# A vision tower on one core: the second stage's attention product turned and spread over four array tiles, squares on ScalarE, bias rows split in the first stage, the last weight fold at its end

## The reference

```python
h = patches(x) @ W.T + b                                    # 768 -> 256
u = layernorm(h); Bu = (u @ W_B.T + b_B) * dt
xs[t] = exp(-exp(log_A) * dt) * xs[t-1] + Bu[t]             # scan over the 196 patches of an image
h = h + xs @ W_C.T + b_C + u @ W_D.T + b_D
x = layernorm(h)
# attention over the 64 images at each patch position, 4 heads of 64
y1 = ln(x + softmax(q @ k.T / 8) @ v @ out_proj.T + ob) * g1 + be1
gates = softmax(y1 @ wg); e = argmax(gates)                 # 8 experts, at most S/8 tokens each, in token order
moe = gate * ((y1 @ w1[e] + b1[e]) @ w2[e] + b2[e])         # 0 for a token past its expert's capacity
out = h + ln(y1 + moe) * g2 + be2
```

## Time and profile before

| | before |
|---|---|
| median of three runs | 1286.43 us (1283.87 to 1287.28) |
| profiled execution | 1285.87 us, span 1284.0 us |
| TensorE busy | 1183.7 us, 92% |
| VectorE busy | 1010.5 us, 79% |
| GpSimd busy | 857.0 us, 67% |
| ScalarE busy | 720.8 us, 56% |
| mean granted TensorE clock | 0.972 |
| stages in the span | first to 547.85, second to 1086.73, third to 1284 |

### The profile page before, as it was taken

The page is one execution under the profiler, slowest core; times in us unless marked ns, Lnnn a source line. Parts: engine busy times, 40 slices in busy tenths (PEclk is TensorE's granted clock), DMA queues, the critical chain, the costliest instruction groups (busy, mean ns, idle before and its releaser), DMA issues. The chain is left out here.

```text
span 1284.0 us, 37111 instructions
## 1 busy us (share of the span) xinstructions
PE 1183.7 (92%) x11134; PEld 1086.1 (85%) x11135; DVE 1010.5 (79%) x2957; ACT 720.8 (56%) x1518; POOL 857.0 (67%) x1159
## 2 busy tenths in 40 slices
PE   1999999999999999749999999999999984999994
PEld 1999999999999999749999999999999973666662
DVE  4688888888888888705778877877788776699997
ACT  3455566566565655415555555555555540678885
POOL 1566666666666666373777777777777773378887
PEclk9999999999999999978999999999999996999997
DMA  7435555545454542211333333333233325788882
GB/s 221 165 126 157 173 155 177 164 146 172 141 184 149 179 148 90 91 42 39 113 104 110 107 107 102 110 105 110 98 111 107 110 92 157 207 236 241 238 235 93
DMA packets 97304, 180.11 MB, mean 140 GB/s; under 512 B 12319, under 2 KB 62753, under 8 KB 96226
## 3 DMA queue, kind: packets, MB, share of 16 engines
q1 hardware_dynamic: 82500, 138.66, 36.0%
q0 software_dynamic: 13312, 39.75, 8.3%
q10 hardware_dynamic: 1440, 1.07, 0.3%
HBM read 112.69 MB, written 67.80 MB: 141 GB/s over the span
## 5 line engine op out<-in xcount | busy, mean ns | idle before, releaser
L528 POOL TENSOR_TENSOR xl<-xf,xh 128x512 fp32r<-128x512 f32 x141 | 183.8, 1332 | 178.0 <-ACT xh L447 178.0
L311 PE MATMUL ps_h<-wh,xh 128*128 128x256 f32 x588 | 166.3, 283 | 4.9 <-DVE xl L669 4.9
L311 PE MATMUL ps_h<-wh,xl 128*128 128x256 f32 x588 | 166.1, 282 | 0.0
L311 PE MATMUL ps_h<-wl,xh 128*128 128x256 f32 x588 | 165.3, 281 | 0.0
L1061 POOL DMA_INDIRECT bins<-rows,slot_i x98 | 109.8, 1120 | 72.8 <-DVE rows L1172 54.0
L1462 POOL DMA_INDIRECT out<-res,c_idx x106 | 123.8, 1168 | 43.3 <-issue 21.4
L947 ACT ACTIVATE q<-b,cols_c 128x256 f32<-128x256 f32 x98 | 41.1, 471 | 158.8 <-PE ps_v L1291 155.1
L311 PE MATMUL b<-x2h,wh 128*128 128x256 f32 x392 | 120.6, 308 | 2.8 <-DVE x2l L1078 2.8
L1610 PE MATMUL c_ps_y<-w,yt 128*128 x424 | 117.9, 401 | 3.3 <-ACT yt L1409 1.7
L311 PEld LDWEIGHTS ps_h<-wh,xh 128*128 128x128 f32 x588 | 111.4, 189 | 5.7 <-DVE xl L669 5.7
L311 PEld LDWEIGHTS ps_h<-wh,xl 128*128 128x128 f32 x588 | 111.4, 190 | 0.0
(11 more groups left out here) (282 smaller groups left out, 4258.0 us busy)
## 6 DMA issues: line engine op xcount, KB each, us to landing
xf<-xt SPq DMA_DIRECT2D x49, 768.0 KB, 5.4
row<-bins SPq DMA_DIRECT2D x106, 257.5 KB
h_dram<-h1b SPq DMA_DIRECT2D x49, 256.0 KB, 5.4
x_dram<-x2o SPq DMA_DIRECT2D x49, 256.0 KB, 5.6
x<-x_dram SPq DMA_DIRECT2D x98, 128.0 KB, 2.8
rows<-h_dram SPq DMA_DIRECT2D x98, 128.0 KB
w1s<-w1t SPq DMA_DIRECT2D x8, 1024.0 KB, 6.8
w2s<-w SPq DMA_DIRECT2D x8, 516.0 KB, 5.9
```

What stands on the lines that cost most here:

```text
L311: last = nc.tensor.matmul(out_ps, a, b, start=(i == 0), stop=(i == len(terms) - 1))
L528: last = nc.gpsimd.tensor_tensor(xl[:, p, part], xf[:, p, part], xh[:, p, part].bitcast(F32), ALU.subtract)
```

## The change

First stage:
- The last expert's fold leaves steps 42 to 45 and stands behind TensorE's last step, with ScalarE's copy behind it.
- `fold_bias` splits each bias row on VectorE as it is made; the eight-row split on GpSimd in the second stage goes, and the ones in va.
- `gate_weights` runs in step 49 instead of 51, in xf instead of w1s. TensorE's part stands in its steps 50 (`gate_first`) and 51 (`gate_second`), the splits in the steps 51 and 52 of VectorE and ScalarE.
- The carried columns are NC = 10 instead of 8: the ninth has weights -1/D, so the products also give minus the mean of z.

Second stage:
- `attend` is turned: v is stationary, the numerators move, the output is features by tokens and needs no turn_o. Tile order (a, t) = (0,0), (1,1), (0,1), (1,0); both head halves and both positions, so all four 64x64 tiles. `scores` also writes to all four, in two banks.
- The numerators are summed and normalised before they are transposed (`normalise`).
- bn_stats and bn_aggr go; `squares` on ScalarE sums (z - mean)^2.
- The order of stages on four engines is new.

```diff
-QS, OS = 3 * D + NE, D + NE
+NC = NE + 2
+QS, OS = 3 * D + NC, D + NC
...
 # first stage, ScalarE
-                    if k.slot(FOLD) == 4 and k.valid(FOLD * NE):
+                    if k.slot(FOLD) == 4 and k.valid(FOLD * (NE - 1)):
...
-                    if isinstance(k.t, int) and k.c == NG + 3:
+                    if isinstance(k.t, int) and k.c == NG + 2:
                         act.wait_ge(turned, 1)
                         nc.scalar.activation(wo_t[:], ps_f[:].rearrange("p (t c) -> p t c", t=FT), ACT.Copy).then_inc(turned_out, 1)
...
+                    if isinstance(k.t, int) and k.c == NG + 3:
+                        act.wait_ge(wog_out, 1)
+                        nc.scalar.activation(gate_part(wh, W_OUT + D, OS), wog[:], ACT.Copy).then_inc(g_hi, 1)
                 run(act, step, 0, NG + 5, 6, 42, FOLD)
+                act.wait_ge(fold_ps, NE)
+                nc.scalar.activation(w12[:, NE - 1, :], ps_f[:], ACT.Copy).then_inc(fold_out, 1)
 # first stage, VectorE: fold_bias, step
                         v.tensor_tensor(row, ps_fb[:], row, ALU.add).then_inc(fb_out, 1)
+                        wait(dve, fb_out, e + 1)
+                        v.tensor_copy(two, row).then_inc(fb_split, 1)
+                        wait(dve, fb_split, e * 4 + 1)
+                        v.tensor_tensor(row, row, two.bitcast(F32), ALU.subtract).then_inc(fb_split, 1)
+                        wait(dve, fb_split, e * 4 + 2)
+                        v.tensor_scalar(row, row, half[:, 1:2], None, ALU.mult).then_inc(fb_split, 1)
+                        wait(dve, fb_split, e * 4 + 3)
+                        v.scalar_tensor_tensor(two, two.bitcast(F32), half[:, 0:1], row, ALU.mult,
+                                               ALU.add).then_inc(fb_split, 1)
...
+                    if isinstance(k.t, int) and k.c == NG:
+                        gate_weights()
                     if isinstance(k.t, int) and k.c == NG + 2:
-                        gate_weights()
+                        gate_low()
 # first stage, TensorE
-                    if k.valid(FOLD * NE):
+                    if k.valid(FOLD * (NE - 1)):
                         fold(k)
                     if k.back(2).valid(NG):
                         inputs(k.back(2))
...
+                    if isinstance(k.t, int) and k.c == NG + 1:
+                        gate_first()
+                    if isinstance(k.t, int) and k.c == NG + 2:
+                        gate_second()
+                run(pe, step, 0, NG + 4, 6, 42, FOLD)
+                for c in range(FOLD):
+                    fold(At(0, FOLD * (NE - 1) + c, FOLD))
 # second stage, ScalarE
+                def squares(m):
+                    wait(act, Q["z"], m.n() + 1)
+                    wait(act, Q["lg"], m.n() + 1)
...
+                    for s in range(2):
+                        A(dev[:, s, :], z[:, s, :], ACT.Square, bias=minus_mean[:, s:s + 1],
+                          accum_out=sq[:, s:s + 1]).then_inc(Q["zsq"], 1)
...
-                    for m, stage in ((k.back(2), v_out), (k.back(2), xg_out), (k.back(5), e_log),
-                                     (k.back(2), lambda m: qk_out(m, "k_ps", kk, FT, "k_out")),
-                                     (k.back(1), lambda m: qk_out(m, "q_ps", q, 0, "q_out")), (k.back(3), o_hi),
-                                     (k.back(2), exps), (k.back(4), z_norm), (k, x_hi), (k.back(2), et_out)):
+                    for m, stage in ((k.back(3), et_out), (k.back(4), squares), (k.back(3), o_hi), (k.back(2), exps),
+                                     (k.back(1), lambda m: qk_out(m, "q_ps", q, 0, "q_out")), (k.back(5), e_log),
+                                     (k.back(1), lambda m: qk_out(m, "k_ps", kk, FT, "k_out")), (k.back(4), z_norm),
+                                     (k.back(1), xg_out), (k.back(1), v_out), (k, x_hi)):
 # second stage, GpSimd
-                    for m, stage in ((k.back(3), y1), (k.back(1), add_const), (k, add_bias), (k.back(3), count),
-                                     (k.back(2), rstd), (k.back(2), centre), (k.back(3), send)):
+                    for m, stage in ((k.back(4), y1), (k.back(4), send), (k, add_const), (k, add_bias), (k.back(2), rstd),
+                                     (k.back(2), centre), (k.back(3), count)):
 # second stage, VectorE
+                def normalise(m):
+                    wait(dve, Q["exp"], m.n() + 1)
+                    v.tensor_reduce(es[:], eb[:].rearrange("p (c m) -> p c m", m=L), AX_X, ALU.add).then_inc(Q["esm"], 1)
+                    wait(dve, Q["esm"], m.n() + 1)
+                    v.reciprocal(rinv[:], es[:]).then_inc(Q["rinv"], 1)
...
+                    v.tensor_tensor(en[:].rearrange("p (c m) -> p c m", m=L), eb[:].rearrange("p (c m) -> p c m", m=L),
+                                    rinv[:].unsqueeze(2).to_broadcast([P, 2 * H, L]), ALU.mult).then_inc(Q["en"], 1)
...
-                    for m, stage in ((k.back(5), gates), (k.back(3), o_lo), (k.back(4), logits), (k.back(4), top_logit),
-                                     (k.back(4), expert), (k.back(4), scaled), (k, x_lo), (k.back(3), residual),
-                                     (k.back(3), mean), (k.back(3), gate_sum), (k.back(2), o_norm), (k.back(4), place),
-                                     (k.back(1), softmax), (k.back(3), shift)):
+                    for m, stage in ((k.back(5), gates), (k.back(2), normalise), (k.back(4), expert),
+                                     (k.back(3), residual), (k.back(3), gate_sum), (k, x_lo), (k.back(1), softmax),
+                                     (k.back(4), place), (k.back(4), scaled), (k.back(2), o_lo), (k.back(3), logits),
+                                     (k.back(3), shift), (k.back(3), top_logit)):
 # second stage, TensorE: scores, attend, step
-                        for t in range(2):
-                            for hh in range(H):
-                                b, a = hh // 2, hh % 2
+                        for b in range(FT):
+                            for a, t in ((0, 0), (1, 0), (0, 1), (1, 1)):
+                                g = a ^ t
                                 r, c = slice(a * HD, (a + 1) * HD), slice(b * G + s * P + t * L, b * G + s * P + (t + 1) * L)
-                                to = (s * 2 + b) * P + t * L
-                                last = mm(ps_s[a * L:(a + 1) * L, to:to + L], q[r, c], kk[r, c], start=True, stop=True)
+                                to = (s * 2 + b) * L
+                                last = mm(b_v[g * L:(g + 1) * L, t, to:to + L], q[r, c], kk[r, c], start=True, stop=True)
...
-                        for hh in range(H):
-                            for t in range(2):
-                                r, c = slice(t * L, (t + 1) * L), (s * 2 + hh // 2) * P + (hh % 2) * L
-                                last = mm(ps_o[r, s, hh * HS:(hh + 1) * HS], et[r, c:c + L], va[r, p, s, hh, :],
+                        for b in range(FT):
+                            for a, t in ((0, 0), (1, 1), (0, 1), (1, 0)):
+                                r, c = slice(t * L, (t + 1) * L), (s * 2 + b) * P + (a ^ t) * L
+                                to, f = (b * 2 + s) * L, b * P + a * HD
+                                last = mm(ps_o[a * HD:(a + 1) * HD, t, to:to + L], va[r, p, s, f:f + HD], et[r, c:c + L],
                                           start=True, stop=True)
...
-                    for m, stage in ((k.back(1), values), (k, turn_x), (k.back(2), turn_e), (k.back(3), project),
-                                     (k.back(2), attend), (k, queries), (k.back(4), rank), (k.back(1), scores),
-                                     (k.back(2), turn_o), (k, keys)):
+                    for m, stage in ((k.back(1), queries), (k.back(1), keys), (k.back(1), values), (k.back(3), project),
+                                     (k, turn_x), (k.back(2), turn_e), (k.back(1), scores), (k.back(2), attend),
+                                     (k.back(4), rank)):
```

More of the change, by code:

```diff
@@ L21 @@
 H, HD = 4, 64
-HS = HD + 1
 NE, FF = 8, 1024
@@ L785, in fold_sum, with gate_first, gate_second @@
                         nc.tensor.matmul(ps_fb[:], ones_2[:], acc[:], start=True, stop=True).then_inc(fb_ps, 1)
+                mm, ps_g = nc.tensor.matmul, ps_h[0]
+                def gate_first():
+                    pe.wait_ge(fold_out, NE - 1)
+                    pe.wait_ge(h_done, 2 * NG)
+                    pe.wait_ge(pre_in, 3)
+                    for t in range(FT):
+                        for i in range(FT):
+                            last = nc.tensor.transpose(ps_f[:, t * D + i * P:t * D + (i + 1) * P], wo[:, i, t * P:(t + 1) * P], ident[:])
+                    last.then_inc(turned, 1)
+                    pe.wait_ge(pre_in, 6)
+                    for t in range(FT):
+                        mm(ps_g[:, FT * NC:(FT + 1) * NC], ones_f[:], gg[:, t, :], start=(t == 0), stop=(t == FT - 1))
+                    for t in range(FT):
```

(10 more changed lines are left out.)

178 lines of the change are left out of this document (66 added, 112 removed).

## The result

The changed kernel takes 1272.31 us (median of four runs, 1270.78 to 1273.86) against 1285.61 us before: a ratio of 0.990, with a 95% interval of 0.988 to 0.991. It is faster by 13.3 us where 37 were forecast.

What follows compares the result with a forecast made beforehand. TensorE's own order was taken to bound the looped part, at 9.895 us a group. The terms +4-15.5-22-4 = -37.5 on 1285.87 gave 1248.4, with 0.56 for the median 1249 us; eight in ten: 1234 to 1266.

Steps and rivals of the forecast that it cites:

- the end of the first stage: First stage's last steps up to the first x2 load: loss of 4 us, load at about 551.9 against 547.85.
- The fold as a trade: Last expert's fold: TensorE loses 6.1 us in steps 42 to 45 and gets them back uncovered behind the last outputs.
- The start of the second stage: First to ninth transpose: bias rows off GpSimd remove the 8.16 us wait for x2; gain 15.5 us.
- The looped step: The second stage's 40 looped groups: step falls from 9.895 to 9.34 us, gain 22 us.
- rival A: Looped step: tiles overlap well, attend 0.8, step 9.1, total 1235; far end step 8.9, about 1226; chance 0.18.
- The drain: Second stage's last groups: shorter path from attend to projection without turn_o and the scaling; gain 4 us.
- B: Looped step: the wait before attend takes the whole step gain, step 9.85, total about 1271; chance 0.13.
- C: Looped step: the new tile order loses the overlap, products 2.0 us, step 11.05, total about 1326; chance 0.04.
- D: Looped step: square is outside Exp's table, so tables load twice a step, near 10.8, total about 1310; chance 0.03.

Runs made afterwards that it cites:

- e1: The changed kernel with the VectorE splits of the first stage undone, GpSimd splitting all bias rows at the start of the second stage as before: 1256.19 us.
- e2: The changed kernel with the same four split operations for each expert issued behind the two scans of the next step instead of ahead: 1274.96 us.
- e13: The changed kernel with GpSimd subtracting only one third of the low half of x in the first stage: 1256.00 us.
- e4: The changed kernel with one VectorE operation for each bias split instead of four, ScalarE making the high half and the scaled sum: 1248.52 us.
- e6: e4's kernel with the last expert's fold back in steps 42 to 47: 1251.40 us.
- e9: e8's kernel with scores and attend running one tile diagonal after the other, one switch in a set: 1233.18 us.
- e11: e8's kernel with an added wait that holds GpSimd's x2b until VectorE's product of pos and oh is done: 1250.41 us.
- e12: e8's kernel with GpSimd's x2b ordered behind rstd and the small gate instructions of its step: 1292.34 us.
- e3: The changed kernel with an added wait meant to hold GpSimd's low-half subtraction until the scans are done: 1269.23 us.
- e8: e4's kernel with gate_weights a step later, gate products behind the last outputs, and the last fold in parts in steps 49 to 52: 1239.82 us.
- e7: e4's kernel with scores and attend alternating only one diagonal's two tiles at a time, in groups of four products: 1249.78 us.

## Why the prediction was wrong

**The step that failed** is the last sentence of the end of the first stage: "The bias splits of the seven other experts (1.7 us each) stand in fold steps where VectorE has about 1.4 us spare a step and the next steps take the rest: 0, at most 3." They cost 22.7 us (e1: 574.86 against 552.20; that holds the last expert's too, which the forecast had in its +4). The own time was right (1.5 measured, 1.7 forecast), and so was the spare time as a sum (1.4 forecast, 1.5 a step in e1). What failed is that the splits were priced at their own time alone, as if it could fill any idle time of VectorE. They shift what follows them into GpSimd's subtraction, where an instruction stands for up to 1.4 us; VectorE is then busy 5.4 us more for each expert, and six steps take 2.7 us more. Durations of the rows of before were taken as fixed; e2 and e13 show that they hold for one alignment of two engines. That the forecast's 1249 came out in e4 does not save this step: e4 is another kernel.

**The end of the stage**, +4: with the splits made cheap, the first load is at 553.92, forecast 551.9 (e4). gate_second's wait was forecast at 3.6 us and is 3.29; gate_weights was put ahead of ul rightly. The fold as a trade: right (e6).

**The start of the second stage**, -15.5: -15.1 (-16.7 by the forecast's own cut). The wait of 8.16 us at the third transpose is gone, as said. The wait that is left, 5.16, is that of the first transpose for the first load, and it was 5.89 before:

```profile
579.04 1.12 PE L1244 MATMUL ps_o<-ident,x 128*128 128x128 f32 x4 [5.16 <-DMA x<-x_dram]
594.91 0.60 PE L1244 MATMUL ps_o<-ident,x 128*128 128x128 f32 x4
```

x2b(0) ends 11.2 us after the first transpose (forecast 10.1) and the third transpose starts 15.9 after it (forecast 15.0). The clock is a part that the forecast did not name: before, TensorE's granted clock was back at 0.50 from 573 to 585, around the 8.16 us of idle time, and in the changed kernel it stays at 1.00 from 588 on. And e1 shows that the splits on GpSimd were 9.5 of the gain, not all of it.

**The looped step**, 9.34: 9.32 (372.88 over 40). The mean is right by luck: one of its parts is not. TensorE's timeline of the changed kernel, from a rank to the next scores:

```profile
790.40 0.18 PE L1325 MATMUL ps_z<-oh,before 128*128 128x8 bf16 x1
796.73 0.60 PE L1244 MATMUL ps_o<-ident,x 128*128 128x128 f32 x4
797.65 0.65 PE L1293 MATMUL b<-ident,en 128*128 128x128 f32 x4 [0.32 <-DVE en L1134]
798.23 0.69 PE L1315 MATMUL ps_v<-k,q 64*64 64x64 f32 x32
```

The products take 0.69, not 1.0 to 1.08: rival A's mechanism, four tiles, and e9 supports it. From attend to attend the short step takes 8.71, even less than rival A's 8.9. But every second step takes 1.2 us more (from turn_x to turn_x the two are 9.04 and 9.64), and VectorE's product of pos and oh stands in it until GpSimd's x2b ends, at 792.52:

```profile
791.06 1.50 DVE L1204 TENSOR_TENSOR pos<-pos,oh 128x16 f32<-128x16 f32 x1
```

```profile
791.21 1.31 POOL L1066 TENSOR_TENSOR x2b<-x,rows_c 128x512 f32<-128x512 f32 x1
```

The product started 0.15 us before x2b, while the short addition xg (791.03 to 791.27) ran; beside x2b alone it takes 0.48 on average, in the other steps. Which of the two additions holds it, the rows don't say. Two errors of opposite sign met: products cheaper than forecast, and a collision that was not in it. That this collision is what makes the long steps long is argued from these rows and e9, and not shown: in e11 the product was short in every step and the mean step grew. Attend does wait where the forecast said, for x2l; it enters 2.1 us after turn_x in the short steps and 3.0 in the long.

**The drain**, -4: -3.0 (-1.6 from the 49th transpose on). From the last attention product to its projection it takes 3.24 us (1041.71 to 1044.95) instead of 5.55; the forecast had 2.6 and more for VectorE's order.

**Rivals.** B (et in ScalarE's queue takes the gain) did not occur: in the loop attend waits for x2l. C (order loses the overlap) is refuted by 0.69. D is refuted: one table load in the start of the second stage, none in the loop, squares 0.50 us each. The page of the Trainium skill that the prediction cites for D names no set that holds square, so that "by its rule there is no load" was my inference; the trace agrees with it.

## What to carry to other kernels

Before work is added to VectorE, look at what GpSimd does just after it: in this case instructions with two SBUF inputs, however small, and copies too (e2), that slid into a GpSimd instruction of 128x512 cost up to that instruction's rest each, and spare time in the sum over a step said nothing of it. To move one of them away by a wait or by order can move the collision to the next (e11, e12), so measure the step and not the instruction; and look in the trace whether an added wait ever held (e3). Small bookkeeping was cheaper on ScalarE, which had time left (21 us of stage time with three operations an expert fewer on VectorE, e4). The fold, the constants and the gate products that left the loop did best when kept off the last group's chain (e8, 9 us for the three moves together).

## What the runs showed of the hardware

- A 2x256 copy took 0.28 us beside an idle GpSimd (changed kernel) and 1.32 beside its subtraction (e2); a subtraction of two SBUF tensors 0.41 and 1.40.
- A 128x16 product of two SBUF tensors took 0.175 us beside GpSimd's 128x2 root in the 38 steps where they met (e9), and 1.49 where it began beside a short GpSimd addition and a 128x512 one followed (changed kernel, 20 cases).
- A set of 32 instructions of 64x64 took 1.15 on two diagonal tiles, 0.98 with both diagonals one after the other (e9), 0.74 in groups of four products (e7), 0.69 with four tiles in turn.
- A square with its sum on ScalarE is two instructions, 0.50 us and 0.19 us to read the sum.
